# Weights prepared one stage ahead, and row sums over key halves that GpSimd has added, in a two-layer graph attention kernel

## What is computed

```python
# layer 0: 8 heads of 32, x is 64 x 256 x 256, adj holds 0 or 1
attn = softmax(q @ k.T / sqrt(32))                  # over the 256 key nodes
out  = sum((attn * (adj == r)) @ v_r for r in range(4))
x    = layernorm(x + out @ Wo + bo)
x    = layernorm(x + gelu(x @ W1 + b1) @ W2 + b2)   # 256 -> 1024 -> 256

# layer 1: 8 heads of 32
e    = leaky_relu(q @ k.T, 0.2)
attn = softmax(where(adj > 0, e, -9e15))
h    = layernorm(attn @ v)
out  = layernorm(concat([h, x]) @ Wffn.T) + x
```

## Time and profile before

| | |
|---|---|
| median of 3 runs | 3339.35 us (3338.1 to 3341.52) |
| the profiled execution, its own time | 3339.18 us |
| its span from first to last record | 3337.4 us |
| PE busy | 3127.1 us, 94% of the span |
| DVE busy | 2341.9 us, 70% |
| ACT busy | 2011.8 us, 60% |
| GpSimd busy | 1316.3 us, 39% |

### The profile page before, as it was taken

How to read it: one execution, slowest core, us unless ns; L and a number is a source line. 1 busy time by engine, 2 the same in 40 slices (tenths; PEclk the granted TensorE clock), 3 DMA queues, 4 the chain that set the end, 5 groups by cost and what they waited for, 6 DMA issues and landing times. The chain is left out here.

```text
span 3337.4 us, 77256 instructions
## 1 busy us (share of the span) xinstructions
PE 3127.1 (94%) x29189; PEld 2102.4 (63%) x29189; DVE 2341.9 (70%) x6791; ACT 2011.8 (60%) x3726; POOL 1316.3 (39%) x1252
## 2 busy tenths in 40 slices
PE   4999999999999949999999948999999999999996
PEld 2666666666666526666666626676676776677764
DVE  5888888888888835555555535777777777777773
ACT  2666656666666535655555515666676666666764
POOL 0455555555555523443444311333333333333333
PEclk9999999999999969999999969999999999999998
DMA  3444444444444311111111123444444444444431
GB/s 119 133 135 140 140 134 136 139 141 134 134 140 140 98 67 39 51 39 52 51 51 51 39 94 112 129 135 132 128 135 130 134 133 128 128 130 136 132 121 46
DMA packets 291038, 365.93 MB, mean 110 GB/s; under 512 B 31713, under 2 KB 199521, under 8 KB 290657
## 3 DMA queue, kind: packets, MB, share of 16 engines
q1 hardware_dynamic: 289216, 359.25, 34.9%
...
## 5 line engine op out<-in xcount | busy, mean ns | idle before, releaser
L1816 ACT ACTIVATE b_prob<-b_score_t 128x512 f32<-128x512 f32 x512 | 304.1, 594 | 372.6 <-PE b_score_t L2093 366.7
L2006 DVE CUSTOM_DVE_ANT_0 b_junk<-b_score,b_mask 128x256 bf16<-128x256 f32 x1024 | 390.4, 418 | 189.3 <-issue 182.9
L2424 DVE TENSOR_TENSOR f_gl<-f_act,f_gh 128x512 f16<-128x512 f32 x256 | 244.5, 956 | 288.3 <-ACT f_act L2354 288.3
L1883 POOL TENSOR_TENSOR b_nw_root<-b_nw_var,b_minus_halves 128x2 f32<-128x2 f32 x128 | 89.9, 702 | 847.8 <-DVE b_nw_neg_mean L1956 847.8
L1361 DVE TENSOR_TENSOR a_linked<-a_prob,a_mask 128x1024 f32<-128x1024 f32 x256 | 356.2, 1392 | 2.8 <-ACT a_prob L1188 2.7
L2349 ACT ACTIVATE f_gh<-f_up,f_b 128x512 f16<-128x512 f32 x256 | 175.5, 686 | 278.5 <-PE f_up L2465 278.4
L1188 ACT ACTIVATE a_prob<-a_score_t 128x1024 f32<-128x1024 f32 x256 | 259.5, 1014 | 109.3 <-PE a_score_t L1439 102.7
L1354 DVE TENSOR_REDUCE a_neg_max<-a_score 128x4 f32<-128x1024 f32 x256 | 306.9, 1199 | 4.8 <-PE a_score L1452 4.7
L1822 ACT ACTIVATE b_score_t<-b_score_t 128x512 f32<-128x512 f32 x512 | 303.2, 592 | 0.3 <-PE b_score_t L2102 0.3
L2463 PE MATMUL f_down<-f_w,f_gh 128*128 128x256 f16 x1024 | 279.1, 273 | 1.0 <-DVE f_gl L2424 1.0
L2464 PE MATMUL f_down<-f_w,f_gh 128*128 128x256 f16 x1024 | 279.1, 273 | 0.0
...
## 6 DMA issues: line engine op xcount, KB each, us to landing
...
```

The costliest lines, as they stand in the source:

```text
L1816: nc.scalar.activation(prob[:, he], score_t[s][:].rearrange("p t n -> p (t n)"), ACT.Exp, scale=ALPHA).then_inc(exp_done, 1)
L2006: last = nc.vector.tensor_tensor_reduce(junk[:, s, it], score[s][:, it], mask[:, i, it], -1.0, 3e38, ALU.add, ALU.min, neg_max[:, i, col:c ...
L2424: nc.vector.tensor_tensor(gl[:, bu[1] % 2, f], act32[:, f % 2], gh[:, bu[1] % 2, f], ALU.subtract).then_inc(low_done, 1)
```

## The change

1. **Row sums over halves.** A new piece of GpSimd, `halved`, adds the two key halves of `prob`: `half_sum` for a pair of heads (128 partitions x 512), four adds per batch, in both attentions. The row sums then take one group of four matmuls per half of the heads in place of two: in the first attention value groups 1 and 3 have 12 matmuls and groups 0 and 2 have 8; in the second attention the sums stand apart (`sums0`, `sums1`), at sub-steps 37 and 39. PE waits there for `half_done`. ACT's exponential of the second attention, which writes `prob` again, waits for it too. Each new `half_sum` waits until the row sums of the batch before have been read.
2. **Second attention, places.** `xh`, `q_hi`, `k_hi`, `v_out` come one sub-step earlier, and stand behind `z1`, `hh` and `z` inside ACT's sub-step where they had stood before them; `q_lo`, `k_lo` and `xl` come ahead of `y` on DVE. The sums are emptied at 39, before the heads, as a piece of its own.
3. **Start of the first attention.** The first x is loaded right behind Wq; PE waits only for what its next piece needs (`ready`): first Wq, then Wk, then Wv at its own sub-step. Wv and Wo are split inside step 1, the maxima wait for the constants. The memset of `stack` goes from DVE to GpSimd, in step 0.
4. **Weights of later stages.** W1 and W2 are loaded and split inside the first attention: W1 loaded in step 3, split by ACT in step 65 (B is 64) and by DVE in step 66; W2 loaded in step 66, split in steps 68 and 69, in the last steps in which batches run out. The five weights of the second attention are loaded in step 2 of feed-forward and split at sub-step 6 of its steps 6 to 11 (`late`); the row `out_row` and the scaling of Wo' come in step 4. The second attention has no weights to load; its memset of `stack` goes to GpSimd too.

```diff
-          "turn_max": 24, "m_hi": 25, "m_lo": 25, "store_m": 26, "ST": 29, "exp": 30, "masked": 31, "values": 34, "res": 36,
+          "turn_max": 24, "m_hi": 25, "m_lo": 25, "store_m": 26, "ST": 29, "exp": 30, "masked": 31, "halved": 32, "values": 34, "res": 36,
...
-            for n, (dst, src) in enumerate(wlist):
-                sp.dma_start(stage[:, n], src.rearrange("(c p) n -> p c n", p=P)).then_inc(w_loaded[n], 16)
+            sp.dma_start(stage[:, 0], w["Wq"].rearrange("(c p) n -> p c n", p=P)).then_inc(w_loaded[0], 16)
+            sp.dma_start(x_sb[:, 0], rows(x_in, (0, 0))).then_inc(x_loaded[0], 16)
+            sp.dma_start(stage[:, 1], w["Wk"].rearrange("(c p) n -> p c n", p=P)).then_inc(w_loaded[1], 16)
             for r in range(2):
                 sp.dma_start(stage_n[:, :, r * D:(r + 1) * D], w["Wv"][r].rearrange("(c p) n -> p c n", p=P)).then_inc(w_loaded[3], 16)
+            sp.dma_start(stage[:, 2], w["Wo"].rearrange("(c p) n -> p c n", p=P)).then_inc(w_loaded[2], 16)
...
+                    if number(t) == 3 and h == 0:
+                        sp.wait_ge(ready, 4)
+                        sp.dma_start(stage_f.rearrange("p (c n) -> p c n", c=DC), wf["W1"].rearrange("(c p) n -> p c n", p=P)).then_inc(ffn_loaded, 16)
+                    if number(t) == B + 2 and h == 4:
+                        sp.wait_ge(ffn_low, 1)
+                        sp.dma_start(stage_f.rearrange("p (c n) -> p c n", c=FF // P), wf["W2"].rearrange("(c p) n -> p c n", p=P)).then_inc(ffn_loaded, 16)
...
+                    if number(t) in (B + 1, B + 4) and h == 7:
+                        part = number(t) > B + 1
+                        act.wait_ge(ffn_loaded, 32 if part else 16)
+                        nc.scalar.activation((w2 if part else w1)[:, 0].rearrange("p c n -> p (c n)"), stage_f, ACT.Copy).then_inc(ffn_high, 1)
```

```diff
+                    if number(t) == 0 and h == 6:
+                        pool.wait_ge(xl_ready, 1)
+                        nc.gpsimd.memset(stack[KQ:P, :, 1], SHIFT).then_inc(stack_set, 1)
+                        pool.wait_ge(stack_set, 1)
...
+                    if due_pair := pair_due(t, h, "halved"):
+                        be, k = due_pair
+                        pool.wait_ge(exp_done, count(be, PAIRS, k + 1))
+                        if k % 2 == 0 and (n := after(back(be, 1), 4, k + 2)) is not None:
+                            pool.wait_ge(values_done, n)
+                        nc.gpsimd.tensor_tensor(half_sum[:, k], prob[:, k, :, 0:N], prob[:, k, :, N:2 * N], ALU.add).then_inc(half_done, 1)
...
+            dve.wait_ge(split_h, 1)
+            nc.vector.tensor_tensor(wq[:, 1], stage[:, 0], wq[:, 0], ALU.subtract).then_inc(ready, 1)
+            dve.wait_ge(split_h, 2)
+            nc.vector.tensor_tensor(wk[:, 1], stage[:, 1], wk[:, 0], ALU.subtract).then_inc(ready, 1)
             dve.wait_ge(prep, PREP)
+            dve.wait_ge(ready, 2)
...
-                        for term in range(3):
+                        if jt == 1:
+                            pe.wait_ge(half_done, count(bv, PAIRS, 2 * c + 2))
+                        for term in range(2 + jt):
                             for a in range(HQ):
                                 pair, e = 2 * c + a // 2, a % 2
                                 part = slice(DH * a, DH * (a + 1))
                                 if term == 2:
-                                    last = nc.tensor.matmul(sums_t[part, 0:N], pick[:, c], prob[:, pair, e, cols], start=k == 0, stop=k == 3)
+                                    last = nc.tensor.matmul(sums_t[part, 0:N], pick[:, c], half_sum[:, pair, e], start=c == 0, stop=c == 1)
```

```diff
-          "offset": 24, "turn_max": 25, "max_rows": 26, "store_m": 26, "ST": 28, "relu": 28, "add": 29, "exp": 29, "values": 33, "res": 45,
...
+          "offset": 24, "turn_max": 25, "max_rows": 26, "store_m": 26, "ST": 28, "relu": 28, "add": 29, "exp": 29, "halved": 31, "sums0": 37, "sums1": 39, "values": 33, "res": 45,
...
+                            act.wait_ge(half_done, n)
...
+            nc.gpsimd.memset(stack[KQ:P, :, 1], SHIFT).then_inc(stack_set, 1)
+            pool.wait_ge(stack_set, 1)
...
+                    if half := half_due(t, h, "halved"):
+                        bv, k = half
+                        pool.wait_ge(exp_done, count(bv, H, 2 * k + 2))
+                        if k % 2 == 0 and (n := after(back(bv, 1), 2, k // 2 + 1)) is not None:
+                            pool.wait_ge(sums_done, n)
+                        pair = prob[:, 2 * k:2 * k + 2]
+                        nc.gpsimd.tensor_tensor(half_sum[:, 2 * k:2 * k + 2], pair[:, :, 0:N], pair[:, :, N:2 * N], ALU.add).then_inc(half_done, 1)
...
+                    for c in range(DC):
+                        if bv := due(t, h, f"sums{c}"):
+                            pe.wait_ge(half_done, count(bv, HALVES, 2 * c + 2))
+                            if c == 0 and (n := after(back(bv, 1), 1, 1)) is not None:
                                 pe.wait_ge(rinv_ready, n)
-                        cols = slice(jt * N, (jt + 1) * N)
-                        for term in range(2):
+                                pe.wait_ge(sums_out, n)
                             for a in range(HQ):
-                                he = HQ * c + a
-                                part = slice(DH * a, DH * (a + 1))
-                                if term:
-                                    last = nc.tensor.matmul(sums_t[part, 0:N], pick[:, c], prob[:, he, cols], start=k == 0, stop=k == 3)
-                                else:
-                                    nc.tensor.matmul(heads_t[part, c], values[:, r4, jt, he * DH:(he + 1) * DH], prob[:, he, cols],
-                                                     start=jt == 0, stop=jt == 1)
-                        last.then_inc(values_done, 1)
+                                last = nc.tensor.matmul(sums_t[DH * a:DH * (a + 1), 0:N], pick[:, c], half_sum[:, HQ * c + a], start=c == 0, stop=c == 1)
+                            last.then_inc(sums_done, 1)
```

```diff
+                if number(t) == 2:
+                    for n, (dst, src) in enumerate(wlist):
+                        sp.dma_start(stage[:, n], src.rearrange("(c p) n -> p c n", p=P)).then_inc(w_loaded[n], 16)
...
+                    if f == 6 and 0 <= number(t) - SPLIT < len(wlist):
+                        n = number(t) - SPLIT
+                        act.wait_ge(w_loaded[n], 16)
+                        if n == HEADS_W:
+                            act.wait_ge(scaled, 1)
+                        nc.scalar.activation(wlist[n][0][:, 0], stage[:, n], ACT.Copy).then_inc(split_h, 1)
...
+                    if f == 6 and number(t) == SPLIT - 2:
+                        dve.wait_ge(row_made, 1)
+                        nc.vector.tensor_copy(late["out_row"][:], turn[0][:, 0:D]).then_inc(row_out, 1)
+                        for c in range(DC):
+                            last = nc.vector.tensor_scalar(stage[:, HEADS_W, c], stage[:, HEADS_W, c], late["vcol"][:, 0, c:c + 1], None, ALU.mult)
+                        last.then_inc(scaled, 1)
+                    if f == 6 and 1 <= number(t) - SPLIT <= len(wlist):
+                        n = number(t) - SPLIT - 1
+                        dve.wait_ge(split_h, n + 1)
+                        nc.vector.tensor_tensor(wlist[n][0][:, 1], stage[:, n], wlist[n][0][:, 0], ALU.subtract)
```

340 lines of the change are left out of this document (174 added, 166 removed).

## The result

The changed kernel takes 3487.07 us (median of four executions), against 3338.88 for the kernel before on the same chip: 1.0441 times as long, with a 95% interval of 1.0421 to 1.0462. One of the four took 4737.78 us at a mean granted clock of 0.61; it is in the median and not in the ratio. The forecast was 3352. It is slower, as forecast, but by 148 us in place of 13. Its profiled execution took 3488.27 us (span 3486.5), and the two profiled executions differ by 149.1 us, which divides as follows. A period is the time from one `a_hl` (GpSimd) to the next in the first attention, from one `b_z<-b_hs` (ACT) to the next in the second; the steady part is 58 and 59 of them.

A forecast was written before the change was run, and what follows sets the result against it. GpSimd's chain to `a_hl` was taken to bound the first attention, PE feed-forward and the second attention. From 3339.2 us: -17 + 66 + 8 - 13 - 13 - 18 = +13, or 3352 us; own range 3335 to 3375, overall 3290 to 3400.

The forecast's parts named there:

- The first attention's loop: First attention: pair 3's add ahead of `a_hl` lengthens the GpSimd chain 1.2 us, period 18.75; +66 us (50 to 83).
- rival D: First attention: PE's longer wait before each projection drops its clock, about 1.7 us a fall; +94, 3446 us; chance 0.06.
- there PE waits anyway: First attention: PE time saved before the end of GpSimd's chain does not shorten the loop; no gain counted.
- The second attention's bound: Second attention, steady: PE is the bound, loses 0.88 us of work, gains 0.3 per batch; -18 us (-52 to +5).
- by itself it would just keep up: Second attention: the chain from DVE's `b_qk` multiply to the next `far` matmul would match a PE 0.88 us shorter.
- PE's gain: Both attentions: dropping two of four row-sum groups saves PE 0.88 us per batch, 0.44 per group.
- The collision with the multiply: Second attention: the add k=2 runs when DVE wants its two-input multiply; DVE waits about 0.65 us.
- The reckoning base: Second attention, steady: 59 batches at a period of 20.04 us before the change.
- Rival C: Second attention gains nothing or loses: +0.3 us a batch instead of -0.3; 3388 us; chance 0.14.
- The tail: First attention's tail: W1 and W2 splits, plus 3.5 us for the add in the last five batches; +8 us (4 to 12).
- The starts: Stage starts with fewer weights to await: first attention -17 us, feed-forward -13, second attention -13.
- "hidden" memset: Second attention's start: the memset moved to GpSimd costs nothing, its next operation not being needed for 30 us.

The follow-up runs named there:

- pair-3 add behind `a_hl`: Changed kernel with the first attention's GpSimd half-sum add of pair 3 directly behind `a_hl` instead of ahead of it; 3328.69 us.
- full sums, dummy add: Changed kernel; first attention: four row-sum groups, no half sums, 128x512 dummy GpSimd add ahead of `a_hl`; second: no adds, row sums left out; 3319.74 us.
- small dummy: Changed kernel; first attention: pair 3's add behind `a_hl`, 128x256 dummy GpSimd add ahead of it; second: two half-sum adds held back; 3376.79 us.
- after, with filler: Changed kernel; first attention: 16 extra PE matmuls during the wait for `a_hl`; second: no half-sum adds, row sums left out, an extra ACT wait; 3415.09 us.
- weights alone: Kernel before with only the change's weights part (starts and splits); row sums, tables and order of both attentions as before; 3298.42 us.
- `affine` moved: Changed kernel with the first attention's `affine` (`a_z`, `a_z_out`) three sub-steps later, behind `a_hl` on GpSimd, all adds kept; 3342.06 us.

## Why the prediction was wrong, and where it was right

**The first attention's loop** was right in mechanism, place and size: chain of the earlier trace rows, 1.22 us per batch where 1.2 stood, 18.76 us where 18.75 stood, and the runs with the add moved and with the dummies in its place confirm it. The add took its turn behind `a_linked` and `a_hl` then none, as the earlier trace rows suggested that one of them would.

**The clock** was the step that failed, and the largest term: 82 of the 135 us. It stood there as rival D, with 0.06, priced at 1.7 us a fall (measured 1.6) and +94. What was wrong was the weighing of the earlier trace rows: I let one gap of 3.62 us without a fall outweigh one of 2.07 with half speed behind it. The trace of before had more to say. The gap of 2.07 was the third in a row of its kind, some 13.5 us apart, and behind the two before it the four score matmuls took 1.04 us as well:

```profile
42.65 1.04 PE L1452 MATMUL a_score<-a_stack 96*128 96x256 f16 x4 [2.62 <-DMA a_stack<-qk_scratch]
...
56.14 1.04 PE L1452 MATMUL a_score<-a_stack 96*128 96x256 f16 x4 [2.12 <-DMA a_stack<-qk_scratch]
```

Of the six gaps of 2.0 to 2.7 us that this trace has with the clock up, five ended in a fall (the other two near 2018 and 2040 us), and one, of 2.10 near 1176, did not. The lengths of the same wait in otherwise like loops tell more still (200 to 1080 us; the length in most batches, by the median):

| run | PE's wait per batch, us | clock |
|---|---|---|
| before | 0.34 | never down |
| pair-3 add behind `a_hl` | 1.0 | never down |
| full sums, dummy add | 1.33 | never down |
| small dummy | 1.57 | never down |
| after | 2.22 | down in most batches (52 long periods of 58) |
| after, with filler | 0.48 | never down |

So what I wrote as two effects that leave each other alone, an add that lengthens the loop and sums that PE saves beside it ("there PE waits anyway"), work together: the saved matmuls shorten nothing and lengthen the stop of PE. With the full sums it was 1.33 us and would be 1.54 with the changed kernel's longer chain (0.21); the 0.69 us that PE saves bring it to the 2.22 at which the clock falls. No run has this wait at a length between 1.57 and 2.2 us in most batches, and the length of a stop alone does not decide: in the run with `affine` moved five stops of 1.99 to 3.26 us had no fall. Why six batches escaped is not shown.

**The second attention's bound** was the other wrong step: +27 in place of -18. "PE is the bound" rested on its busy share of 99% and on a chain without slack from 2619.15 to 2624.36, of which I said that "by itself it would just keep up". I had priced the chain but not closed it to a loop. Closed, it is 20.04 us long, as long as PE's own work in a batch that waits for nothing, and half of it VectorE's. So PE's gain could not come through: with all collisions gone the period is 0.31 shorter, and PE's gain was mis-sized besides (0.69 measured in the first attention, 0.88 reckoned from the 0.54 us of one group). The collision with the multiply was named and sized (0.65, measured 0.48); the one with `b_neg_some` (0.55) was not looked for, since I compared the adds with the one wide instruction and not with the small ones. The reckoning base was off too: the mean period before is 20.34, not 20.04, in part because some batches wait for the stack (9.9 of the 18 us that the 59 periods are longer). Rival C had the right sign.

**The tail** cost 21.9 and not 8. The weights' share was 6.5 where 4.3 stood, and the rest 15.4 where 3.5 stood for the adds: with the pair-3 add moved the tail is 103.7, 9 above the run with the weights alone, and 6 more go with the pair-3 add's old place. How these divide between adds and clock was not tried.

**The starts** were right within 3 us in the first two stages (-14.0 and -12.1). In the first, the memset on GpSimd took 6.92 us and was hidden (GpSimd then waited 1.40 us for its next input), where on VectorE it had stood ahead of the first matmul. In the third it was -24.3 in place of -13: the weights alone gave -9.4, short of 13 by 3.6, of which 1.7 us are `b_linked`, which stood behind the "hidden" memset (2.13 us long in that run, 3.87 in the changed kernel) while PE waited for it; the other 1.9 are not explained. The rest came with this attention's own changes, which I had priced at nothing at its start.

The Trainium skill's rule on the shared pair of ports (SBUF — State Buffer, "Who interferes with whom") would have found more than I took from it. `b_neg_some` has two inputs from SBUF; `b_linked` and `b_mask` have one and are `tensor_scalar`, of which the page says that it can enter a mode that contends too. This case agrees: 0.42 us became 1.50 beside an add and 3.87 beside a memset.
